# Attention rows laid out channel-major inside a half row, with the rows of Wo loaded in the matching order

## The reference, cut to what matters

```python
def _L0_attn_ref(x, Wq, Wk, Wv, Wo, betas, memory0, z0):
    H, DK, DV, LSEG = (16, 64, 64, 128)
    q_all = (x @ Wq).reshape(B, n_seq, LSEG, H * DK)        # k_all, v_all likewise
    def step(carry, seg):
        M, Z = carry
        q = qs.reshape(B, H, LSEG, DK)                       # k, v likewise
        scores = jnp.where(mask, -jnp.inf, jnp.einsum('bhid,bhjd->bhij', q, k) * scale)
        att_dot = jnp.einsum('bhij,bhjv->bhiv', jax.nn.softmax(scores, axis=-1), v)
        att_mem = sq @ M / (sq @ jnp.swapaxes(Z, -2, -1))    # sq = elu(q) + 1, sk = elu(k) + 1
        M_new = M + jnp.einsum('bhld,bhlv->bhdv', sk, v)
        att = gate * att_mem + (1.0 - gate) * att_dot
        out = att.reshape(B, LSEG, H * DV) @ Wo
        return ((M_new, Z_new), out)
x = x + _layernorm(_L0_attn_ref(_layernorm(x), ...))
x = x + _layernorm(_L0_ffn_ref(_layernorm(x), ...))          # three cycles of the coupling network
```

## Time and profile before

| | |
|---|---|
| median of 3 runs | 1279.06 us (1278.69 to 1281.06) |
| the profiled execution: its own time | 1277.61 us |
| its span, first to last instruction | 1275.8 us |
| mean granted TensorE clock | 0.941 of 2.4 GHz |
| busy: PE, DVE, ACT, POOL | 1084.4, 855.4, 611.2, 584.1 us |
| busy share: PE, DVE, ACT, POOL | 85%, 67%, 48%, 46% |

### The profile page before, as it was taken

One profiled execution on the slowest core, in us unless ns is written; L12 is line 12 of the kernel. 1 busy time (PEld: TensorE's weight loads), 2 busy tenths in 40 slices (PEclk: granted clock), 3 DMA queues, 4 the chain that ended last, 5 costly groups with the idle time before them and its releaser, 6 DMA issues.

```text
span 1275.8 us, 20673 instructions
## 1 busy us (share of the span) xinstructions
PE 1084.4 (85%) x7172; PEld 755.4 (59%) x7172; DVE 855.4 (67%) x1492; ACT 611.2 (48%) x1291; POOL 584.1 (46%) x715
## 2 busy tenths in 40 slices
PE   3798989897888899878889888989888888999971
PEld 1475767664767676646666666676767675433331
DVE  4868686866686868656877687768686752434365
ACT  4354444444353535434545454535353553566662
POOL 2145454554454545444545454545454552322266
PEclk9999998988999989989999999999999988999995
DMA  5000000000000000000000000000000010300014
GB/s 161 20 10 9 10 9 10 10 11 9 10 9 9 9 10 10 10 11 2 17 10 9 9 10 9 10 10 9 9 2 9 1 28 1 140 0 0 1 33 99
DMA packets 14842, 24.02 MB, mean 19 GB/s; under 512 B 5264, under 2 KB 7056, under 8 KB 14224
## 3 DMA queue, kind: packets, MB, share of 16 engines
q1 hardware_dynamic: 14736, 22.63, 5.8%
HBM read 13.97 MB, written 8.65 MB: 18 GB/s over the span
## 4 chain that ended last, share of the span: by engine, by line
PE 49%; DVE 29%; issue 11%; ACT 7%; POOL 2%; DMA 1%; SPq 0%; DVEq 0%; POOLq 0%; ACTq 0%
PE ps L1109 12%; PE ps L1214 9%; DVE arena L814 7%; PE ps L1327 6%; PE ps L1167 5%; DVE arena L911 3%; PE ps L1340 3%; ACT arena L574 3%; PE ps L1172 3%; PE ps L1154 3%; DVE arena L758 2%; DVE arena L845 2%; DVE arena L824 2%; PE ps L1199 2%; DVE arena L828 2%
## 5 line engine op out<-in xcount | busy, mean ns | idle before, releaser
L1109 PE MATMUL ps<-arena 128*128 128x512 f16 x1152 | 274.0, 390 | 6.0 <-DVE arena L790 4.2
L574 ACT ACTIVATE arena<-ps,arena 128x128 f32<-128x128 f32 x512 | 139.3, 384 | 223.3 <-DVE arena L835 223.1
L814 DVE STREAM_TRANSPOSE arena<-ps 128x1024 f32<-128x1024 f32 x96 | 190.2, 1983 | 43.8 <-PE ps L1109 43.8
L1109 PEld LDWEIGHTS ps<-arena 128*128 128x128 f16 x1152 | 113.8, 100 | 131.8 <-issue 18.7
L418 POOL TENSOR_TENSOR arena<-arena 128x256 f32<-128x256 f32 x128 | 93.0, 727 | 161.7 <-DVE arena L845 161.7
L1167 PEld LDWEIGHTS ps<-arena 128*128 128x128 f32 x1024 | 134.8, 200 | 25.6 <-issue 17.3
L1167 PE MATMUL ps<-arena 128*128 128x65 f32 x1024 | 137.5, 280 | 13.2 <-DVE arena L845 11.8
L402 POOL TENSOR_TENSOR arena<-arena 128x512 f32<-128x512 f32 x64 | 81.3, 1270 | 125.5 <-ACT arena L567 125.5
L1214 PE MATMUL ps<-arena 128*128 128x256 f32 x544 | 122.0, 382 | 0.3 <-ACT arena L586 0.3
L388 POOL TENSOR_TENSOR arena<-arena 128x2 f32<-128x2 f32 x50 | 9.8, 196 | 238.8 <-DVE arena L754 238.8
L1214 PEld LDWEIGHTS ps<-arena 128*128 128x128 f32 x544 | 102.0, 190 | 16.1 <-ACT arena L586 1.4
(11 more groups left out here) (109 smaller groups left out, 1873.5 us busy)
## 6 DMA issues: line engine op xcount, KB each, us to landing
x_rows<-arena SPq DMA_DIRECT2D x17, 256.0 KB, 2.0
arena<-in_L_attn_x_dram SPq DMA_DIRECT2D x64, 64.0 KB
arena<-x_rows SPq DMA_DIRECT2D x4, 1024.0 KB, 8.0
out_dram<-arena SPq DMA_DIRECT2D x32, 128.0 KB, 2.9
arena<-in_L_attn_Wq_dram SPq DMA_DIRECT2D x1, 1024.0 KB, 12.2
arena<-in_L_attn_Wk_dram SPq DMA_DIRECT2D x1, 1024.0 KB, 14.4
arena<-in_L_attn_Wv_dram SPq DMA_DIRECT2D x1, 1024.0 KB, 17.4
arena<-in_L_attn_Wo_dram SPq DMA_DIRECT2D x1, 1024.0 KB, 13.0
```

Source lines behind the costliest of these rows:

```text
L574: last = act.activation(Pr[:, par, j, :], s_bank[:, par, j * P:(j + 1) * P], ACT.Exp, bias=negm[:, par, j:j + 1])
L814: dve.transpose(dst[:, d0:d0 + 32, :], bank.rearrange("p w (d c) -> p d w c", c=C)).then_inc(x_free, 1)
L1109: last = pe.matmul(bank[:, w, :], xc[:, lx, k, w * P:(w + 1) * P], W16[lw][:, k, i, :], start=(n == 0), stop=(n == 5))
```

## The change

The 16 units of a half row now lie together in `nat`, and the 64 channels are the outer index: a number of unit `c` and channel `e` stands at word `16 e + c` of its half row, where it stood at `64 c + e`. The block transposes of L911 read as before and write 16 words in a run, at a step of one word, then 16 words in the other half row. PE's transposes still take 128 words that lie together, which are now 8 channels of 16 units. So partition `16 e' + c` of block `j` stands for row `64 c + 8 j + e'` of Wo, and Wo is loaded in that order by 8 transfers, one for each `e'`, on 16 partitions each, in place of one on 128. The semaphore's waits count 7 transfers more (192 for 80). The same numbers are multiplied and summed, in another order.

```diff
-        nat = alloc(2 * H * DK).rearrange("p (w c e) -> p w c e", w=2, c=C)
+        nat = alloc(2 * H * DK).rearrange("p (w e c) -> p w e c", w=2, c=C)
...
-                sp.dma_start(Wo_sb, Wo.rearrange("(j p) n -> p j n", p=P)).then_inc(c_in, 16)
+                for e in range(8):
+                    sp.dma_start(Wo_sb[C * e:C * e + C], Wo.rearrange("(c j e) n -> e c j n", j=8, e=8)[e]
+                                 ).then_inc(c_in, 16)
...
-                act.wait_ge(c_in, 80)
+                act.wait_ge(c_in, 192)
...
-                        dve.transpose(nat.rearrange("p w c e -> p e w c")[:, 32 * e:32 * e + 32, :, :],
+                        dve.transpose(nat.rearrange("p w e c -> p e w c")[:, 32 * e:32 * e + 32, :, :],
                                       att.rearrange("p (u e) -> p e u", u=UNITS)[:, 32 * e:32 * e + 32, :]
                                       ).then_inc(nat_done, 1)
...
-                                            nat[:, i // 2, 2 * j:2 * j + 2, :].rearrange("p c e -> p (c e)"),
+                                            nat[:, i // 2, 8 * j:8 * j + 8, :].rearrange("p e c -> p (e c)"),
...
-                pe.wait_ge(c_in, 80)
+                pe.wait_ge(c_in, 192)
```

## The result

| | before | after |
|---|---|---|
| median of 8 runs | 1278.88 us (1277.38 to 1281.06) | 1269.84 us (1260.22 to 1275.33) |
| profiled execution, span | 1277.61, 1275.8 us | 1260.22, 1258.4 us |
| its mean granted clock | 0.941 | 0.959 |

The ratio is 0.9921, 95% interval 0.9904 to 0.9939: 9.0 us faster. The forecast was 12.4 us: from 1279.06, the median then known, to 1266.7. The profiled execution after the change is the fastest of its eight, 9.6 us under their median, so what its trace gained (17.4 us) isn't what the change is worth. The runs of the changed kernel spread over 15 us, those of before over 4.

A forecast was written before the change was run, and what follows sets the result against it. No engine is full; the chain hops between PE and DVE, with PE waiting behind L911 each step. 9.5 (transposes) + 2.9 (clock) + 0 (Wo's load) = 12.4 us less, 1266.7 us as median; range 1254 to 1279.5.

The forecast's parts named there:

- The path: In all 16 steps PE waits before L1138 behind DVE's L911, so a shorter L911 passes to PE undiminished.
- L911's length: DVE's block transpose L911 falls from 2246 ns to 1.95 us, 0.59 us a step, 9.5 us in all.
- The read-bound rival: The strided read of att sets L911's pace: it stays at 2.15 to 2.25 us, time about 1278; chance 0.24.
- The write-bound rival: The write at a step was what cost: L911 falls to 1.4 to 1.6 us, time about 1251; chance 0.12.
- The cap: Up to 1.48 us a step passes to PE before L1138; ACT's result leaves DVE's L823 1.68 us.
- The slower rival: Breaks between L911's write runs of 16 cost, 0.2 us an instruction: 1285.5 us; chance 0.07, a late start-up included.
- The clock: Shorter PE waits before L1138 remove half of the clock falls behind them, seen in six of 16 steps: 2.9 us.
- The load of Wo: At the start, eight transfers add 4.8 us of issuing on SP, mostly hidden in queue waiting, the rest covered: 0.

The follow-up runs named there:

- the load of Wo alone: The kernel before with one edit, Wo loaded by eight transfers on 16 partitions each, in the old order: 1280.97 us, ratio 1.0017.
- DVE's time given back: The changed kernel with one needless DVE reduction of 512 f16 numbers behind L913 in each of the 16 steps: 1282.10 us.

## Why the prediction was right

- **The path.** Right. PE waited behind DVE in each step, the wait fell from 28.3 to 19.5 us, and putting DVE's time back took the gain away.
- **L911's length.** 1940 ns against 1950 predicted, from L814 and L790 as nearest rows. The steps' 16 waits went down by 26.2 - 17.4 = 8.8 us against the sum's 9.5, 0.55 a step for 0.59. The read-bound rival (0.24) falls: the read is as dear alone as the write alone, and what the change removed was the second strided side. The write-bound rival (0.12) falls with it: 1.20 us needs both sides dense.
- **The cap.** Right: with 1.20 us transposes PE's wait is zero and ACT comes in late by 0.25.
- **The slower rival.** Falls: a run of 32 and two runs of 16 take the same.
- **The clock.** Right in kind: the slow groups behind the waits went from six to none, and to one or none in the changed kernel's two repeats; waits of 1.54 us and more brought eight back. But the term counted only the falls right behind this wait. Others went elsewhere in the steps: windows from pair to pair at PEclk 1.00 were none, one and one of 16 in the three traces with the long waits, and eight, four and five in the three of the changed kernel. So the term isn't a number that the prediction could add up from its rows: what is left of the measured 9.0 us, after 8.8 for the waits and 2.1 back for the load, is 2.3 us. It is near the 2.9 forecast, in a kernel whose runs spread over 15, and that nearness is in part luck.
- **The load of Wo.** This step failed in size: taken as 0, it measured 2.1 us by itself. That most of the 4.8 us of issuing would go into the queue's waiting was wrong: `memory0`'s first transfer left SP 5.1 us later. The cover on ACT held all the same: L541 waited 0.82 us, and 1.24 us of idle time were left behind it. But the weights landed later beside the eight parts (from issue, in the two first traces: Wq 13.8 us for 12.2, Wk 19.3 for 14.4, Wv 22.7 for 17.4), and ACT's first conversion of them, of Wq or of Wk, is on the chain at the start. The prediction had considered this for Wq alone, with the wrong sign, and the 12.17 us moved 3.3 MB (275 GB/s over them) and not its 4. By which of them the 2.1 us come isn't settled.
- **The two rules of the Trainium skill** (SBUF — State Buffer, "Door 1: The DMA port swizzle"). That every access in a new 16-byte line pays is borne out on DVE: 0.75 us for either strided side; for POOL's write at a step of 32 words it was 12 ns. That the slower side would then set the pace alone, which the prediction put beside the rule and which would have left no gain, is not: two strided sides took 0.3 us more than one. Its warning of loads on 16 partitions pointed the right way; that the ports are why the weights landed later was not tested.

Sum: 8.8 + 2.3 - 2.1 = 9.0 us, against 9.5 + 2.9 - 0 = 12.4. The 8.8 and the 2.1 are measured, the 2.3 is what is left, so that the two sides meet is no proof of it.

## What to carry to other kernels

When a transpose or copy on DVE moves data between two layouts, look at the step of both sides: one strided side cost 0.75 us for 1024 f32 numbers, the second 0.3, so curing one of two gave less than a third of what curing both gives, and the side worth curing is the one whose producer can scatter for nothing (here POOL, 12 ns). Read on the chain how much of it passes and what is next. A load cut into parts to permute rows may be paid where the other loads of the start are waited for, and not at its own semaphore: here it cost 2.1 us though its own wait was covered. Where the clock's falls differ from run to run, one profiled execution may be 10 us off its median, so the sum is tested by single edits and not by two traces.

## What the hardware showed that was not expected

- Longer waits of PE go with more falls of the clock behind them. Over the three traces with waits of 1.47 to 2.17 us at this place (the kernel before, the load of Wo alone, DVE's time given back), 20 of 48 steps went on at a lower clock; in those with the short waits of the changed kernel and its two repeats, 1 of 48, and that one behind a wait of 1.57 us. Over all eight traces with one strided side it is 4 of 128, each behind one of the longest waits of its trace. The length alone doesn't decide: waits of 1.79 us here, and one of 2.19 elsewhere in the step, were followed by no fall.
- POOL wrote 256 numbers at a step of 32 words in 737 ns, densely in 725. DVE paid 0.75 us for 1024 at a step of 64.
- Eight transfers of 128 KB each held SP's queue for 14 to 15 us at the start. The single one of 1 MB held it for 0.72, but the transfer behind it then for 10.19. Behind the other loads, the eight took 5.13 us.
